# Scan stage of a decoder layer: softplus as one activation per pair, the product u moved, and another split of the products with C

## The chip, the cores and the metric

One NeuronCore of a Trainium2 chip. Its engines run their own instruction streams and meet at semaphores: TensorE (PE), VectorE (DVE), ScalarE (ACT), GpSimd (POOL), and SyncE (SP), whose queue starts most DMAs. The metric is the device time of one execution in microseconds (us).

## The reference

The layer is a Mamba block, then cross-attention, then a feed-forward block, for 16 sequences of 224 rows and 512 columns. The change is in the Mamba block:

```python
x = silu(causal_conv(hidden @ W_in)[first half])      # 1024 channels
x_dbl = x @ W_x                                       # 64 columns for dt, 16 for B, 16 for C
dt = softplus(x_dbl[..., :64] @ W_dt + b_dt)
A = -exp(A_log)                                       # 1024 x 16
# over the 224 rows of a sequence:
h = exp(dt_t[..., None] * A) * h + (dt_t * x_t)[..., None] * B_t[:, None, :]
y_t = einsum('bdn,bn->bd', h, C_t)
out = ((y + x * D) * silu(z)) @ W_out
```

## The kernel before

`mamba_phase` handles one sequence b after the other (B = 16). The scan of one sequence is cut into 32 **slots** g, four to each of the 8 channel tiles; a slot holds 32 channels times 16 states on 128 partitions and four rows of states. So there are 512 slots, and 32 of them are called a **window** here. Each engine's program is one loop over slots, and it works strictly in its own order. While the scan of sequence b runs, the same window prepares sequence b+1 (and the beginning of b+2): the tables FIRST, SECOND and LATER say in which slot each step is put. LATER is given relative to slot 4 of the sequence's own scan, so an entry `at` stands in slot 36 + at of the window before (from -36 up).

The work of one slot g:
- GpSimd, `inputs` (L811): hs[g % 8] = u times B, one product of 128x896. The ring has RING = 8 buffers; the buffer of slot g is free when TensorE has summed the tile of slot g-8, so `inputs(g)` waits for that sum.
- ScalarE, `decays` (L443): four exponentials into one of two PSUM buffers (DA = 2), one slot ahead.
- VectorE, `scan_states` (L700): the scan, and for three of four slots the product with C (L707). For every fourth slot GpSimd makes that product in `times_c` (L818), five slots later in its own order.
- TensorE, `sum_states` (L323), at every fourth slot: it sums the finished tile over the states. In its order it is followed by that slot's other matmuls.

The starts of these sums are used as marks: **M1** is the sum at slot 4 of a window (its tile is slots 0 to 3), M2 that at slot 8, up to M8, which is the next window's slot 0. M(k+1) can't come before all products with C of tile k are done, nor before TensorE has worked through what its program puts between the two.

The preparation in a usual window, by slot: x_dbl (L354) at 3 after silu of x (L518, ScalarE, slot 2); dt matmuls (L363) at 6, 8, 10, 12; for each pair of tiles a softplus in parts: Abs, Relu, Exp and Square on ScalarE (L542 to L547, `softplus_parts`), two instructions on VectorE (L687, L690, `softplus_series`), Ln and Relu on ScalarE (`softplus_log`), and at 18 one sum for all tiles on GpSimd (L823, `softplus_sum`); u = dt times x (L829, `scale_x`) at 20; store_du at 21; the gate of the sequence before (L834) on GpSimd at 8; out_proj (L375) at 11 and 13; x and z projections (L345) at 19, 21, 23, ... 31 and at 1; the transposes of the next h (L334) at 17. Between them stand 11 units of the key and value projections (L400 for keys, L404 for values), by the list `usual`. All these matmuls but the sums share three PSUM banks in turn (`take_bank`): a bank is free when its reader has run. ScalarE takes a projection out one slot after TensorE's slot (`kept_at`, and the entries tap and keep_z); `older_taps` (L674) on VectorE adds the other taps of the convolution.

SyncE's loop is in slot order too. In slot s (a multiple of 4) it loads a tile of dt and u, spread over the partitions (rep, L895), for the tile two after; the load of a sequence's first tile, in slot 24, waits for the whole store of dt and u (`du_out`).

## Time and profile before

| | |
|---|---|
| median of 3 runs | 3470.42 us (3466.92 to 3472.16) |
| the profiled execution | 3465.96 us |
| its span, first to last instruction | 3464.6 us |
| mean granted TensorE clock | 0.969 of full speed |
| busy: PE, DVE, ACT, POOL | 3157.1, 2651.0, 2391.0, 1805.6 us |

The scan stage fills the first 56% of the span, from the first scan at 84.59 us to the last sums near 1922 us; attention and feed-forward follow and are not touched. In a timeline a row gives the start in us, the duration in us, engine, line, operation, output<-input, the number of merged instructions and, in brackets, the idle time before with what ended it. In the groups of instructions the figures behind the bar are busy us and mean ns of one.

### The profile page before, as it was taken

Reading aid. Unit: us, or ns where it says so; the run is one execution under the profiler, and the core shown is the slowest. Engines: PE = TensorE matmul, PEld = TensorE weight load, DVE = VectorE, ACT = ScalarE, POOL = GpSimd, SP = SyncE. Lnnn points to the kernel's source line nnn. Section 1 sums busy time; section 2 is a strip of 40 time slices with the busy share of each in tenths; the row PEclk is TensorE's granted clock in tenths of the full one; section 3 lists DMA queues with packets and bytes.
Section 4 is the critical chain, followed back from the end, with each engine's and each line's share of the span. In section 5 each row is a group of like instructions: output and inputs, shape, how many; then the busy total and the mean of one; then the engine's idle time right before and its main releaser. Section 6 shows DMA issues by size and latency. Waiting matters only on the chain. (4 is left out here: it accounts for less than half of the span.)

```text
span 3464.6 us, 59578 instructions
## 1 busy us (share of the span) xinstructions
PE 3157.1 (91%) x20736; PEld 2191.5 (63%) x20736; DVE 2651.0 (77%) x4673; ACT 2391.0 (69%) x5339; POOL 1805.6 (52%) x1211
## 2 busy tenths in 40 slices
PE   5789889988899898988899799999999999899999
PEld 4566556665666566655655466666666666578887
DVE  2899999999999999999987577777777777523232
ACT  5778887788777877788775477777777777622222
POOL 2678888888788878887877000000010010055554
PEclk8899999999999999999999899999999999999999
DMA  5576666766676667766566221121121121120110
GB/s 164 158 188 184 179 167 175 192 185 173 154 196 189 169 155 191 194 165 166 165 186 183 87 72 48 65 76 48 53 88 48 53 86 63 52 70 25 36 38 25
DMA packets 286297, 425.01 MB, mean 123 GB/s; under 512 B 28753, under 2 KB 226129, under 8 KB 281394
## 3 DMA queue, kind: packets, MB, share of 16 engines
q1 hardware_dynamic: 278637, 411.44, 42.5%
q10 hardware_dynamic: 7365, 9.77, 0.9%
q8 instruction: 169, 2.77, 0.3%
q14 instruction: 126, 1.03, 0.1%
HBM read 320.12 MB, written 101.02 MB: 122 GB/s over the span
## 5 line engine op out<-in xcount | busy, mean ns | idle before, releaser
L811 POOL TENSOR_TENSOR a_hs<-a_rep,a_bmat 128x896 f32<-128x896 f32 x512 | 1061.7, 2097 | 282.8 <-PE a_yps L323 282.4
L443 ACT ACTIVATE a_states<-a_rep,a_a_neg 128x224 f32<-128x224 f32 x2048 | 794.6, 438 | 82.4 <-DVE a_hs L707 80.8
L700 DVE TENSOR_TENSOR_SCAN a_states<-a_states,a_hs 128x900 f32<-128x900 f32 x384 | 779.9, 2031 | 77.2 <-ACT a_states L443 62.2
L1427 DVE CUSTOM_DVE_ANT_0 b_sc<-sps,early_mask 112x375 f32<-112x375 f32 x1024 | 500.0, 545 | 133.4 <-PE sps L1173 127.4
L1314 ACT ACTIVATE b_sc<-b_sc,b_nmax 112x750 f32<-112x750 f32 x512 | 467.3, 913 | 0.7 <-DVE b_nmax L1433 0.7
L1187 PEld LDWEIGHTS b_tps<-ident,b_sc 112*125 112x125 f32 x3072 | 356.9, 189 | 168.5 <-issue 118.6
L345 PE MATMUL a_work<-early_scan_hT,w_in 128*128 128x224 f32 x2048 | 425.3, 363 | 7.5 <-issue 5.0
L707 DVE TENSOR_TENSOR a_hs<-a_states,a_cmat 128x896 f32<-128x896 f32 x384 | 419.2, 1092 | 13.2
L1187 PE MATMUL b_tps<-ident,b_sc 112*125 112x112 f32 x3072 | 404.2, 281 | 26.5 <-DVE b_pT L1441 21.0
L1567 POOL TENSOR_SCALAR b_x_var<-mv 112x2 f32<-112x2 f32 x16 | 3.4, 214 | 814.7 <-DVE mv L1478 814.7
L345 PEld LDWEIGHTS a_work<-early_scan_hT,w_in 128*128 128x128 f32 x2048 | 396.6, 196 | 49.3 <-issue 42.3
L1322 ACT ACTIVATE b_pT<-b_tps 125x448 f32<-125x448 f32 x512 | 275.6, 538 | 162.5 <-PE b_tps L1187 156.3
L400 PE MATMUL a_work<-ctx,a_wk 128*128 128x250 f32 x1536 | 351.1, 381 | 14.4 <-ACT kv_out L490 14.4
L404 PE MATMUL a_work<-wv,ctx 128*125 128x512 f32 x768 | 353.9, 604 | 9.8 <-ACT kv_out L487 9.4
L323 PE MATMUL a_yps<-a_hs,a_fold 128*32 128x224 f32 x4096 | 244.8, 383 | 114.1 <-POOL a_hs L818 46.1
L400 PEld LDWEIGHTS a_work<-ctx,a_wk 128*128 128x128 f32 x1536 | 291.6, 192 | 65.9 <-issue 17.2
L1820 ACT ACTIVATE c_g<-sps,early_b,early_alpha 128x512 f32<-128x512 f32 x112 | 87.2, 779 | 278.5 <-PE sps L1746 272.7
L1856 DVE CAST c_gT_hi<-c_g 128x512 fp32r<-128x512 f32 x112 | 66.8, 596 | 276.4 <-ACT c_g L1820 276.4
L700 DVE TENSOR_TENSOR_SCAN a_hs<-a_states,a_hs 128x900 f32<-128x900 f32 x128 | 258.9, 2023 | 25.2 <-ACT a_states L443 25.1
L323 PEld LDWEIGHTS a_yps<-a_hs,a_fold 128*32 128x32 f32 x4096 | 133.5, 115 | 225.3 <-DVE a_hs L707 96.7
L375 PE MATMUL a_work<-a_w_out,a_yT 128*112 128x512 f32 x512 | 238.8, 622 | 24.6 <-DVE early_du L690 24.6
L1894 POOL TENSOR_TENSOR c_gT_lo<-c_g,c_gT_hi 128x512 fp32r<-128x512 f32 x112 | 146.5, 1310 | 208.9 <-DVE c_gT_hi L1856 208.9
(199 smaller groups left out, 4966.4 us busy)
## 6 DMA issues: line engine op xcount, KB each, us to landing
a_rep<-du_scratch SPq DMA_DIRECT2D x512, 224.0 KB, 5.7
w_in<-W_in_dram SPq DMA_DIRECT2D x128, 512.0 KB, 4.5
du_scratch<-early_du SPq DMA_DIRECT2D x16, 1792.0 KB, 11.5
ctx<-ctxT_dram SPq DMA_DIRECT2D x48, 500.0 KB, 6.3
v_scratch<-kv_out SPq DMA_DIRECT2D x96, 250.0 KB
k_scratch<-kv_out SPq DMA_DIRECT2D x96, 250.0 KB, 4.6
b_keys<-k_scratch SPq DMA_DIRECT2D x8, 1500.0 KB, 9.2
b_v<-v_scratch SPq DMA_DIRECT2D x8, 1500.0 KB
```

Of the source, the lines that this page charges most:

```text
L323: mm = pe.matmul(yps[j * DG:(j + 1) * DG, tile % 2 * L:(tile % 2 + 1) * L], fold[:], hs[(G4 * tile + j) % RING][:, q, 1:ROW], start=(q == ...
L345: mm = pe.matmul(work[:, bank, j * L:(j + 1) * L], w_in[unit % WINS][:, k, j * P:(j + 1) * P], hT[:, k, :], start=(k == 0), stop=(k == KD ...
L400: mm = pe.matmul(work[:, bank, j * WIDE:(j + 1) * WIDE], wk[:, k, (2 * half + j) * P:(2 * half + j + 1) * P], keys[:, k, :], start=(k == 0 ...
L404: mm = pe.matmul(work[0:KC, bank, :], keys[:, k, half * KC:(half + 1) * KC], wv[:, k, :], start=(k == 0), stop=(k == KD - 1))
L443: e = act.activation(rows(states[:, g % DA, :])[:, q, 1:ROW], rep[tile % REPS][:, j, 0, :], ACT.Exp, scale=a_neg[:, g % SLOTS, q:q + 1])
L700: dve.tensor_tensor_scan(state if g % G4 else whole, state, whole, 0.0, ALU.mult, ALU.add).then_inc(S["scan"], 1)
L707: dve.tensor_tensor(hh[:, :, 1:ROW], rows(states[:, g % DA, :])[:, :, 1:ROW], cmat[b % 2][:], ALU.mult).then_inc(S["hc"], 1)
L811: pool.tensor_tensor(hs[g % RING][:, :, 1:ROW], rep[tile % REPS][:, j, 1, :].unsqueeze(1).broadcast_to([P, Q, L]), bmat[b % 2][:], ALU.mul ...
L1187: mm = pe.transpose(tps[0:KC, bank, c * TT:(c + 1) * TT], sc[buffer_of(m // 2)][:, 2 * (m % 2) + head, chunk * KC:(chunk + 1) * KC], ident ...
L1314: act.activation(scores, scores, ACT.Exp, scale=-1.0, bias=nmax[:, block % 3, j:j + 1], accum_out=esum[:, block % 2, head:head + 1]).then_ ...
L1322: act.activation(place(m, pair), transposed(tile), ACT.Copy).then_inc(S["pt_act"], 1)
L1427: dve.tensor_tensor_reduce(out=sc[buffer_of(block)][:, j, cols], in0=sps[0:TT, j, 0:HALF], in1=mask[:, block % 2, cols], scale=-1.0, scala ...
```

## The change

Softplus becomes one ScalarE activation for each pair of tiles, from PSUM into dt. In a usual window all four stand in slot 21, the dt matmuls in slots 18, 18, 21 and 21; the table of activations is switched before the first and back after the last. The parts on VectorE and the sum on GpSimd are gone. u stands in slot 26, silu of z in 25, store_du in 24; z projections and their copies one slot later. Of eight products with C GpSimd takes three (slots 0, 4 and 6 of every eight) instead of two; the third stands four slots after its scan in GpSimd's order, and VectorE's scan of such a slot writes straight to the ring buffer. The key and value units keep their number, with some slots moved. For the first sequence softplus, skip, u and store_du come earlier, and the first table switch goes straight to softplus. The semaphores and the counts that are waited for follow (`products`, `pool_products`).

```diff
@@ -241,23 +238,22 @@
             "row_stats": [-65], "squares": [-60], "guess": [-58], "gains": [-54], "h": [-53], "hT": [-51], "keep_hT": [-50],
             "load_x": [-67, -66, -48, -47], "load_z": [-46, -45, -28, -28], "x": spaced(-49, 1), "tap": spaced(-48, 1),
             "older_taps": spaced(-47, 1), "z": [-30, -29, -24, -23], "keep_z": [-29, -28, -23, -22], "residual": [-19],
-            "silu_x": [-43], "x_dbl": [-42], "xd": [-41], "store_bc": [-41], "dt": spaced(-40, 1), "parts": spaced(-39, 1),
-            "series": spaced(-38, 1), "logs": spaced(-37, 1), "skip": [-32, -31], "spread": [-28], "dt_sum": [-30],
-            "silu_z": [-20], "u": [-28], "store_du": [-27]}
+            "silu_x": [-43], "x_dbl": [-42], "xd": [-41], "store_bc": [-41], "dt": [-40, -40, -40, -39],
+            "softplus": [-39, -39, -39, -39], "skip": [-42, -42], "spread": [-38], "silu_z": [-20], "u": [-38],
+            "store_du": [-37]}
         SECOND = {
             "load": [-20], "row_stats": [-16], "squares": [-15], "guess": [-14], "gains": [-13], "h": [-12], "hT": [-11],
             "keep_hT": [-10], "load_x": [-7, 1, 3, 5], "load_z": [-6, 2, 4, 6], "x": spaced(0, 2), "tap": spaced(1, 2),
             "older_taps": spaced(2, 2), "z": spaced(1, 2), "keep_z": spaced(2, 2), "residual": [9], "silu_x": [9],
-            "x_dbl": [10], "xd": [11], "store_bc": [11], "dt": spaced(12, 1), "parts": spaced(13, 1),
-            "series": spaced(14, 1), "logs": spaced(15, 1), "skip": [18, 19], "spread": [17], "dt_sum": [20],
-            "silu_z": [21], "u": [21], "store_du": [22]}
+            "x_dbl": [10], "xd": [11], "store_bc": [11], "dt": [18, 18, 21, 21],
+            "softplus": [21, 21, 21, 21], "skip": [18, 19], "spread": [17], "silu_z": [25], "u": [26], "store_du": [24]}
         LATER = {
             "load": [-68], "row_stats": [-64], "squares": [-60], "guess": [-58], "gains": [-54], "h": [-53], "hT": [-51],
             "keep_hT": [-50], "load_x": spaced(-52, 4), "load_z": spaced(-50, 4), "x": spaced(-49, 4), "tap": spaced(-48, 4),
-            "older_taps": spaced(-47, 4), "z": spaced(-47, 4), "keep_z": spaced(-46, 4), "residual": [-35], "silu_x": [-34],
-            "x_dbl": [-33], "xd": [-32], "store_bc": [-32], "dt": spaced(-30, 2), "parts": spaced(-29, 2),
-            "series": spaced(-28, 2), "logs": spaced(-27, 2), "skip": [-20, -19], "spread": [-19], "dt_sum": [-18],
-            "silu_z": [-16], "u": [-16], "store_du": [-15]}
+            "older_taps": spaced(-47, 4), "z": spaced(-46, 4), "keep_z": spaced(-45, 4), "residual": [-35], "silu_x": [-34],
+            "x_dbl": [-33], "xd": [-32], "store_bc": [-32], "dt": [-18, -18, -15, -15],
+            "softplus": [-15, -15, -15, -15], "skip": [-20, -19], "spread": [-19], "silu_z": [-11], "u": [-10],
+            "store_du": [-12]}
         when = [FIRST, SECOND] + [{name: [b * SLOTS + BEHIND + at for at in slots_of] for name, slots_of in LATER.items()}
                                   for b in range(2, B)]
 
@@
...
-        usual = (1, 3, 5, 12, 14, 18, 20, 22, 24, 26, 30)
+        usual = (1, 3, 5, 12, 13, 18, 20, 21, 24, 25, 29)
...
@@ -281,9 +277,16 @@
 
         bank_of = {}
 
+        def pool_multiplies(g):
+            return g % (2 * G4) in (0, G4, G4 + 2)
+
         def products(g):
 
-            return (G4 - 1) * (g // G4) + g % G4
+            return 5 * (g // (2 * G4)) + sum(not pool_multiplies(n) for n in range(g % (2 * G4) + 1))
+
+        def pool_products(g):
+
+            return 3 * (g // (2 * G4)) + sum(pool_multiplies(n) for n in range(g % (2 * G4) + 1))
 
         def in_unit(b, name, pair):
 
@@ -314,8 +317,8 @@
                 return bank
 
             def sum_states(tile):
-                pe.wait_ge(S["hc"], (G4 - 1) * (tile + 1))
-                pe.wait_ge(S["hc_pool"], tile + 1)
+                pe.wait_ge(S["hc"], products(G4 * tile + G4 - 1))
+                pe.wait_ge(S["hc_pool"], pool_products(G4 * tile + G4 - 1))
                 if tile % 2 == 0 and tile:
                     pe.wait_ge(S["y"], tile // 2)
                 for q in range(Q):
@@ -435,7 +438,7 @@
                 tile, j = g // G4, g % G4
                 if j == 0:
                     act.wait_ge(S[f"rep{tile % REPS}"], 16 * G4 * (tile // REPS + 1))
-                if g >= DA and (g - DA) % G4 == 0:
+                if g >= DA and pool_multiplies(g - DA):
                     act.wait_ge(S["scan"], g - DA + 1)
                 elif g >= DA:
                     act.wait_ge(S["hc"], products(g - DA))
@@ -516,7 +519,7 @@
                     act.wait_ge(S["du_out"], 16 * b)
                 for half in halves:
                     act.activation(xs[:, half, :], conv[:, half, :], ACT.Silu).then_inc(S["xs"], 1)
-                act.preload_act_table_set("natural_log_exp_and_others")
+                act.preload_act_table_set("natural_log_exp_and_others" if b else "softplus")
 
             def silus_z(b):
                 act.wait_ge(S["z"], PAIRS * (b + 1))
@@ -533,29 +536,16 @@
                 act.activation(xd[0:R, :], work[0:R, bank, 0:L], ACT.Copy).then_inc(S["xd"], 1)
                 act.activation(bc[R:R + 2 * N, :], work[R:R + 2 * N, bank, 0:L], ACT.Copy).then_inc(S["bc"], 1)
 
-            def softplus_parts(b, pair):
-                n = PAIRS * b + pair
-                cols = slice(2 * pair, 2 * pair + 2)
-                view = pair_of_tiles("dt", b, pair)
-                act.wait_ge(S["dt_ps"], n + 1)
+            def softplus(b, pair):
+                act.wait_ge(S["dt_ps"], PAIRS * b + pair + 1)
                 act.wait_ge(S["xs"], 2 * (b + 1))
-                steps.after(act.activation(conv[:, cols, :], view, ACT.Abs))
-                steps.after(act.activation(dt[:, cols, :], view, ACT.Relu))
-                steps.settle()
-                steps.after(act.activation(conv[:, cols, :], conv[:, cols, :], ACT.Exp, scale=-1.0))
-                steps.settle()
-                act.activation(view, conv[:, cols, :], ACT.Square, scale=3.0 ** -0.5,
-                               bias=series_bias[:]).then_inc(S["square"], 1)
-
-            def softplus_log(b, pair):
-                n = PAIRS * b + pair
-                cols = slice(2 * pair, 2 * pair + 2)
-                act.wait_ge(S["part"], n + 1)
-                steps.after(act.activation(conv[:, cols, :], conv[:, cols, :], ACT.Ln, bias=1.0))
-                steps.settle()
-                act.activation(conv[:, cols, :], conv[:, cols, :], ACT.Relu, bias=log_small[:]).then_inc(S["log_part"], 1)
+                act.activation(dt[:, 2 * pair:2 * pair + 2, :], pair_of_tiles("dt", b, pair),
+                               ACT.Softplus).then_inc(S["dt"], 1)
+                if pair == PAIRS - 1:
+                    act.preload_act_table_set("natural_log_exp_and_others")
 
             def skip(b, half):
+                act.wait_ge(S["xs"], 2 * b + half + 1)
                 if b >= 2:
                     act.wait_ge(S["o_ps"], 2 * (b - 1))
                 for m in range(half * M // 2, (half + 1) * M // 2):
@@ -817,14 +785,9 @@
                 pool.wait_ge(S["scan"], g + 1)
                 pool.tensor_tensor(hh[:, :, 1:ROW], hh[:, :, 1:ROW], cmat[b % 2][:], ALU.mult).then_inc(S["hc_pool"], 1)
 
-            def softplus_sum(b):
-                pool.wait_ge(S["part"], PAIRS * (b + 1))
-                pool.wait_ge(S["log_part"], PAIRS * (b + 1))
-                pool.tensor_tensor(dt, dt, conv[:], ALU.add).then_inc(S["dt"], 1)
-
             def scale_x(b):
                 pool.wait_ge(S["skip"], 2 * (b + 1))
-                pool.wait_ge(S["dt"], b + 1)
+                pool.wait_ge(S["dt"], PAIRS * (b + 1))
                 pool.wait_ge(S["xd_ps"], b + 1)
                 pool.tensor_tensor(xs, xs, dt, ALU.mult).then_inc(S["u"], 1)
 
@@ -851,14 +814,13 @@
             for slot in range(slots[0], ALL + 50):
                 if 0 <= slot < ALL:
                     inputs(slot)
-                if 0 <= slot - AHEAD < ALL and (slot - AHEAD) % G4 == 0:
-                    times_c(slot - AHEAD)
+                for g in (slot - AHEAD, slot - AHEAD + 1):
+                    if 0 <= g < ALL and pool_multiplies(g) and (g % G4 == 0) == (g == slot - AHEAD):
+                        times_c(g)
                 for b, _ in due(slot, "squares"):
                     squares_of(b)
                 for b, _ in due(slot, "gains"):
                     gains(b)
-                for b, _ in due(slot, "dt_sum"):
-                    softplus_sum(b)
                 for b, _ in due(slot, "u"):
                     scale_x(b)
                 for b in range(B - 1):
```

## Rows read from the trace of the kernel before

**Rows 1.** page, part 2: busy tenths of VectorE in 40 slices of the span

```profile
DVE  2899999999999999999987577777777777523232
```

**Rows 2.** timeline of TensorE in one window: start us, duration us, engine, line, [idle before]

```profile
907.62 3.24 PE L354 MATMUL a_work<-early_du,early_w_x 128*96 128x224 f32 x16 [0.75 <-ACT early_du L518]
910.79 1.74 PE L323 MATMUL a_yps<-a_hs,a_fold 128*32 128x224 f32 x32
...
915.94 0.92 PE L363 MATMUL a_work<-a_xd,early_w_dt 65*128 65x224 f32 x4
...
923.64 1.74 PE L323 MATMUL a_yps<-a_hs,a_fold 128*32 128x224 f32 x32 [3.35 <-POOL a_hs L818]
...
934.13 7.12 PE L375 MATMUL a_work<-a_w_out,a_yT 128*112 128x512 f32 x16 [3.47 <-DVE early_du L690]
941.18 1.73 PE L323 MATMUL a_yps<-a_hs,a_fold 128*32 128x224 f32 x32
...
952.07 1.73 PE L323 MATMUL a_yps<-a_hs,a_fold 128*32 128x224 f32 x32 [1.34 <-DVE a_hs L707]
...
969.14 2.62 PE L323 MATMUL a_yps<-a_hs,a_fold 128*32 128x224 f32 x32 [3.04 <-issue]
...
982.13 1.74 PE L323 MATMUL a_yps<-a_hs,a_fold 128*32 128x224 f32 x32
983.80 3.65 PE L400 MATMUL a_work<-ctx,a_wk 128*128 128x250 f32 x16
987.28 3.19 PE L345 MATMUL a_work<-early_scan_hT,w_in 128*128 128x224 f32 x16
990.31 3.60 PE L404 MATMUL a_work<-wv,ctx 128*125 128x512 f32 x8
...
996.86 1.74 PE L323 MATMUL a_yps<-a_hs,a_fold 128*32 128x224 f32 x32
```

**Rows 3.** timeline of TensorE, the same product seven windows later

```profile
1703.40 3.24 PE L354 MATMUL a_work<-early_du,early_w_x 128*96 128x224 f32 x16 [0.80 <-ACT early_du L518]
```

**Rows 4.** timeline of GpSimd in the window of group 2

```profile
912.70 2.10 POOL L811 TENSOR_TENSOR a_hs<-a_rep,a_bmat 128x896 f32<-128x896 f32 x1 [2.17 <-PE a_yps L323]
...
919.53 2.08 POOL L811 TENSOR_TENSOR a_hs<-a_rep,a_bmat 128x896 f32<-128x896 f32 x1
921.57 1.93 POOL L818 TENSOR_TENSOR a_hs<-a_hs,a_cmat 128x896 f32<-128x896 f32 x1
...
967.12 1.92 POOL L818 TENSOR_TENSOR a_hs<-a_hs,a_cmat 128x896 f32<-128x896 f32 x1
```

**Rows 5.** costly groups of VectorE in that window: busy us, mean ns, idle before

```profile
L707 DVE TENSOR_TENSOR a_hs<-a_states,a_cmat 128x896 f32<-128x896 f32 x24 | 26.2, 1092 | 0.8
...
L687 DVE SCALAR_TENSOR_TENSOR a_work<-a_work,early_conv 128x448 f32<-128x448 f32 x4 | 2.5, 615 | 0.0
```

**Rows 6.** costly groups of ScalarE in that window

```profile
L543 ACT ACTIVATE early_du<-a_work 128x448 f32<-128x448 f32 x4 | 2.1, 532 | 0.0
...
L518 ACT ACT_TABLE_LOAD x1 | 1.3, 1283 | 0.0
```

**Rows 7.** timeline of TensorE early on, after a longer wait

```profile
124.42 6.06 PE L354 MATMUL a_work<-early_du,early_w_x 128*96 128x224 f32 x16 [6.24 <-ACT early_du L518]
```

**Rows 8.** DMA issues: KB each and median us to landing

```profile
a_rep<-du_scratch SPq DMA_DIRECT2D x512, 224.0 KB, 5.7
...
du_scratch<-early_du SPq DMA_DIRECT2D x16, 1792.0 KB, 11.5
```

**Rows 9.** timeline of the prologue, ScalarE and GpSimd

```profile
44.23 0.55 ACT L542 ACTIVATE early_conv<-a_work 128x448 f32<-128x448 f32 x1 [0.80 <-PE a_work L363]
...
61.99 3.99 POOL L829 TENSOR_TENSOR early_du<-early_du 128x1792 f32<-128x1792 f32 x1
```

**Rows 10.** timeline of TensorE in the last window

```profile
1851.38 1.73 PE L323 MATMUL a_yps<-a_hs,a_fold 128*32 128x224 f32 x32
...
1860.10 1.73 PE L323 MATMUL a_yps<-a_hs,a_fold 128*32 128x224 f32 x32
```

More of the change, by code:

```diff
@@ L16 @@
 NEG_INF_SCALE = -1e9
-LOG1P_SMALL = 2.0 ** -8
 class Memory:
@@ L234, in mamba_phase @@
         n_weights = 11
-        n_const = 6
+        n_const = 4
         def spaced(first, step):
@@ L358, in dt_raw @@
             def dt_raw(b, pair):
-                bank = take_bank(("dt", b, pair), "part", PAIRS * b + pair + 1)
+                bank = take_bank(("dt", b, pair), "dt", PAIRS * b + pair + 1)
                 pe.wait_ge(S["xd"], b + 1)
@@ L638, in scalar_program @@
                     keep_xd(b)
-                for b, pair in due(slot, "parts"):
-                    softplus_parts(b, pair)
-                for b, pair in due(slot, "logs"):
-                    softplus_log(b, pair)
+                for b, pair in due(slot, "softplus"):
+                    softplus(b, pair)
                 for b, _ in due(slot, "silu_z"):
@@ L681, in older_taps @@
                 e.then_inc(S["conv"], 1)
-            def softplus_series(b, pair):
-                cols = slice(2 * pair, 2 * pair + 2)
-                series = pair_of_tiles("dt", b, pair)
-                dve.wait_ge(S["square"], PAIRS * b + pair + 1)
-                steps.after(dve.scalar_tensor_tensor(out=series, in0=series, scalar=13.0 / 16.0, in1=conv[:, cols, :],
-                                                     op0=ALU.add, op1=ALU.mult))
-                steps.settle()
-                dve.scalar_tensor_tensor(
-                    out=dt[:, cols, :], in0=series, scalar=LOG1P_SMALL * (LOG1P_SMALL ** 2 / 3 - LOG1P_SMALL / 2 + 1),
-                    in1=dt[:, cols, :], op0=ALU.min, op1=ALU.add).then_inc(S["part"], 1)
             def scan_states(g):
@@ L762, in vector_program @@
                     dve.tensor_scalar(a_neg[:], a_neg[:], -1.0, None, ALU.mult).then_inc(S["const"], 1)
-                    dve.wait_ge(S["log_small"], 1)
-                    steps.after(dve.tensor_scalar(log_small[:], log_small[:], -1.0, None, ALU.mult))
-                    steps.settle()
                 for b, pair in due(slot, "older_taps"):
                     older_taps(b, pair)
-                for b, pair in due(slot, "series"):
-                    softplus_series(b, pair)
                 for b in range(B):
```

28 lines of the change are left out of this document (11 added, 17 removed).

## Prediction

> **What bounds the kernel now.** I read the page first. Its row of slices shows VectorE busy at 90% or more through the whole scan, slices 3 to 18 of 40 [rows 1]. Taken alone that says: every microsecond taken off VectorE is a microsecond gained. So I went on to the timeline of one window, engine by engine, to see which wait ends last at each mark. One x_dbl starts at 907.62 us and the one seven windows later at 1703.40 [rows 2, 3]: 795.78 / 7 = 113.7 us for a window. The marks inside are the starts of the sums [rows 2]:
>
> M1 910.79, M2 923.64, M3 941.18, M4 952.07, M5 969.14, M6 982.13, M7 996.86.
>
> What ended each stretch is to be read from the idle time in brackets and from what ran just before:
> - M1 to M2, 12.85 us: TensorE idles 3.35 us for GpSimd. The chain is GpSimd's own. Its first product of the stretch starts 1.91 us after the sum did (912.70, the ring buffer comes free); small steps and the gate follow, the next product at 919.53, the product with C from 921.57 to 923.50, and the sum starts at 923.64 [rows 2, 4].
> - M2 to M3, 17.54: TensorE. It waits 3.47 us for a bank that the softplus series on VectorE holds, then out_proj takes 7.12 and ends at the mark.
> - M3 to M4, 10.89: VectorE's last product, with 1.34 of waiting.
> - M4 to M5, 17.07: GpSimd again. Its product with C ends at 967.12 + 1.92 = 969.04, late because the softplus sum and u stand before it on its engine [rows 4].
> - M5 to M6, 12.99, and M6 to M7, 14.73 (M7 to M8 is its like): TensorE without a gap. 14.73 is a sum, two units and two projections [rows 2].
>
> So VectorE ends one of eight stretches, though it looks full. TensorE and GpSimd end most. TensorE couples back within about a slot: ScalarE must take out what TensorE made one slot earlier before it makes the next decays.
>
> **The change part by part**, against the profiled execution (3465.96 us; span 3464.6). From [rows 2]: a key unit takes 3.48 (983.80 to 987.28), a value unit 3.6, so 3.5 each; a projection 3.03 (987.28 to 990.31); a sum 1.67 (982.13 to 983.80); the two dt matmul pairs of one step 0.85 (0.92 with their tail); out_proj 7.1.
>
> VectorE loses four pairs of instructions at 615 ns (the second of each pair is put at the price of the first) and 4 of 24 products at 1092 ns [rows 5]: 4.9 + 4.4 = 9.3 us a window. ScalarE loses 24 activations and gains 4 of the length of a Relu from PSUM, 0.53, with two table loads of 1.28 [rows 6]. GpSimd loses a sum of 4.0 and gains four products of 1.93: +3.7 us [rows 4]. None of that counts by itself; the stretches do:
>
> 1. M1 to M2. Tile 1 is an odd one, so the mark now needs two products on GpSimd, at slots 9 and 10, and between them stands one more `inputs`. The chain grows by 2.07 + 1.93 [rows 4]: 12.85 + 4.0 = **16.85**. No cover is left: TensorE has 1.67 + 2 x 3.5 = 8.7 us of work there and VectorE about 11.5. **+4.0**.
> 2. M2 to M3. The dt matmuls and their bank wait are gone: sum, unit and out_proj give 1.67 + 3.5 + 7.1 = 12.3. But TensorE comes out of a wait of 16.85 - 8.7 = 8.2 us. What that does is seen earlier: after 6.24 us of idling x_dbl took 6.06 us, against 3.24 in the usual window [rows 7, 2], and the sum after 3.04 idle took 2.62 for 1.74. This is the granted clock at its lower level, 1.2 for 2.4 GHz. The loss was 2.8 and 0.9; for 8.2 us I take 2.6, bounds 0 and 5.6 (twice the row, since the wait is longer). 14.9 against 17.54: **-2.6**.
> 3. M3 to M4. VectorE's work falls below, but tile 3 is odd: release of the buffers 1.91, three `inputs`, two products: 1.91 + 3 x 2.07 + 2 x 1.93 = 12.0, against 10.89: **+1.1**. This is a floor for every stretch that ends an odd tile.
> 4. M4 to M5. The softplus sum and u no longer stand in GpSimd's chain. TensorE is next: sum, two units, transposes of 0.9, two dt steps, one projection: 1.7 + 7.0 + 0.9 + 1.7 + 3.1 = 14.4, with 0.6 for banks that wait for ScalarE: 15.0. **-2.1**.
> 5. M5 to M6. Work: sum, two dt steps, z, unit, x: 1.7 + 1.7 + 3.0 + 3.5 + 3.1 = 13.0. The third dt step needs the bank of the first, which the first softplus frees; on ScalarE that is behind a tap of the x projection (1.0), the decays (1.6), the table load (1.28) and the softplus (0.55): 4.6 us after M5 with its latencies, where TensorE is ready at 1.7. So it stands for 3.0, and everything queued behind it (dt, z, unit, x) moves. 16.1 against 12.99: **+3.1**. The table load back costs ScalarE 1.28, and the decays wait, but TensorE is later still.
> 6. M6 to M8 and M8 to M1 stay: the same matmuls, full clock. u has moved to slot 26; there GpSimd has some 3 us to spare in each stretch. store_du in slot 24 holds SyncE until u is done, some 16 us after M5, and what is queued behind it (a w_in load, key and value stores, then rep, which needs the store's 11.5 us and 5.7 of its own [rows 8]) still lands about when the ring asks for it, near M7 + 2. I put it at 0, bounds 0 and +2.
>
> Sum for a usual window: 4.0 - 2.6 + 1.1 - 2.1 + 3.1 = +3.5 against this window's 113.0; against the mean of 113.7, which holds the windows where the clock was low already, +2.8. Thirteen usual windows: **+36**. The last two: each gets step 1 (+4), their matmul work is the same, and in the last the stretch from 1851.38 to 1860.10, 8.72 us [rows 10], rises to the 12.0 of step 3; less about 2 for the lighter steps: **+11**. In the prologue the first softplus starts at 44.23 [rows 9] and four of 0.53 with the last dt step end near 47.3, so u ends at 51.3 instead of 61.99 + 3.99 = 65.98. Not all of the 14.7 us arrives: the z projections, their silu and the next sequence's first steps on ScalarE stand before the first decays. Half is taken, **-7**, bounds -14.7 and 0. First window: 0, bounds -5 and +5.
>
> Total +40: 3466 + 40 = 3506 for such an execution. That execution was 4.5 us below the median of the runs, so **3510**.
>
> A rule that speaks against step 5's size: in the Trainium skill, "ScalarE: Activation LUTs", section "Rules for kernel authors", a switch to a different set is budgeted at about 2.7 us. The trace has 1283 ns for one load [rows 6]. With the page's figure the stand of TensorE would be 1.4 us longer in each window, an estimate of 18 us more in all, 3528; I go by the row.
>
> **The rivals.**
> (a) *The clock costs nothing more than before*, because TensorE's waits only change places. For: the windows before hold low stretches already. Against: 8.2 us is longer than any wait in the usual window, and the work behind it is now what sets M3. Then step 2 is -5.2, the window +0.2 against the mean: 13 x 0.2 + 11 - 7 = +7, **3477**, give or take 15.
> (b) *TensorE doesn't stand in slot 21*, as it is late enough, or ScalarE early enough, to meet the softplus, and the clock holds. Step 5 then gives 13.0 and step 2 12.3, so the window is 2.9 below the mean: 13 x -2.9 + 4 = -34, **3436**. This ends on the other side. Its place is slot 21; with the clock held it decides from the point where that wait is under some 2.5 us, with the loss of step 2 never.
> (c) *VectorE was the bound*: the 90% are true and the waits at the marks only follow it. Then 9.3 us go from 15 windows, 140, and with the prologue 147: **3324**. Against it stands that M2 and M5 end on GpSimd's product to within 0.14 us and M6 and M7 on TensorE without a gap.
> (d) *Slower than forecast*: the rep load of the next sequence comes late (2 us a window) and the clock falls at three waits rather than one (0.9 more twice): 13 x 3.8 = 49, **3559** at the end. It is the tail of the forecast, not a case of its own.
> That softplus isn't one activation, or needs more tables than counted, would show at once in slot 21 and costs 1.28 for each load more.
>
> **How the numbers follow.** Forecast 0.53, (a) 0.24, (b) 0.12, (c) 0.11. The time is the forecast's, 3510. A difference under 0.2% (7 us) is about what a measurement of this kernel can't tell from none. The forecast lies above that with nearly all its chance. (a) spreads 3462 to 3492: a third within 0.2%, a tenth below. So faster 0.12 + 0.11 + 0.03 = 0.26; same 0.09; slower 0.65. For 8 in 10 the range leaves out (c) and the last of (d): **3430 to 3550**.
>
> **What would show it.** In a window of the profile after: M1 to M2 at 16.8 with TensorE idle 8 us for GpSimd's product with C; a granted clock of 0.5 behind it and out_proj or unit stretched; M3 to M4 at 12; M4 to M5 near 15 with no wait on GpSimd; in M5 to M6 a wait of 3 us of the dt matmul for ScalarE; M6 to M8 at 14.7 each; VectorE's share of the scan falling from over 90% to about 85% with the window no shorter. It would be wrong if GpSimd's third product were not in the mark's chain, or if the marks moved together with VectorE's instruction sum.

## The result, and the profile after

The changed kernel takes 3550.39 us (median of 4 runs, 3548.5 to 3551.32) where the kernel before takes 3470.35 (3466.92 to 3472.16, runs on the same chip): ratio 1.0231, 95% interval 1.0213 to 1.0249. That is 80 us slower. The forecast was 3510, with the sign right and half of the size missing; 3550.39 is just above its range.

The page of the kernel after, rows of busy tenths and of the granted clock in 40 slices:

```profile
DVE  2888788878887888788877477777777777622222
...
PEclk8899889988998999899999899999999999999999
```

VectorE has fallen from 9 to 7 and 8 [rows 1], and the clock row has many slices of 8. For the scan, 200 to 1700 us, here is the view of one stretch: us, then busy time (with instruction records) of PE, PEld, DVE, ACT and POOL, then granted clock, DMA share and GB/s. First the kernel after:

```profile
200.00:1700.00 1500.00, 1316.24 (x7369) 906.46 (x7372) 1247.67 (x1078) 1054.96 (x2445) 1235.20 (x708) 0.91 0.66 168
```

The kernel before, the same stretch:

```profile
200.00:1700.00 1500.00, 1346.64 (x7769) 928.35 (x7758) 1419.39 (x1298) 1211.36 (x2799) 1245.21 (x696) 0.96 0.66 177
```

In these 1500 us VectorE is busy 172 us less and ScalarE 156, but part of that is only that fewer windows fit into them. Over the same thirteen usual windows (226.02 to 1703.40 us before, 217.81 to 1770.52 after) VectorE's busy time falls from 1399 to 1289 us, which is 8.5 us a window where 9.3 were forecast, and ScalarE's from 1196 to 1091; the windows take 75 us more. What moved is the clock, 0.96 to 0.91, and the marks. The timeline of TensorE in one window of the kernel after (columns as in [rows 2]):

```profile
934.34 3.24 PE L357 MATMUL a_work<-early_du,early_w_x 128*96 128x224 f32 x16 [0.28 <-ACT early_du L521]
937.51 1.74 PE L326 MATMUL a_yps<-a_hs,a_fold 128*32 128x224 f32 x32
...
954.29 3.21 PE L326 MATMUL a_yps<-a_hs,a_fold 128*32 128x224 f32 x32 [8.03 <-POOL a_hs L786]
957.44 4.90 PE L403 MATMUL a_work<-ctx,a_wk 128*128 128x250 f32 x16
962.18 7.03 PE L378 MATMUL a_work<-a_w_out,a_yT 128*112 128x512 f32 x16
969.14 1.74 PE L326 MATMUL a_yps<-a_hs,a_fold 128*32 128x224 f32 x32
...
981.15 3.05 PE L326 MATMUL a_yps<-a_hs,a_fold 128*32 128x224 f32 x32 [3.22 <-POOL a_hs L786]
...
996.64 1.74 PE L326 MATMUL a_yps<-a_hs,a_fold 128*32 128x224 f32 x32
1001.08 3.36 PE L366 MATMUL a_work<-a_xd,early_w_dt 65*128 65x224 f32 x8 [2.69 <-ACT early_du L542]
1004.23 4.96 PE L348 MATMUL a_work<-early_scan_hT,w_in 128*128 128x224 f32 x16
1009.02 3.60 PE L407 MATMUL a_work<-wv,ctx 128*125 128x512 f32 x8
1012.46 3.19 PE L348 MATMUL a_work<-early_scan_hT,w_in 128*128 128x224 f32 x16
1015.58 1.74 PE L326 MATMUL a_yps<-a_hs,a_fold 128*32 128x224 f32 x32
```

Three waits stand in it: 8.03 us before M2, 3.22 before M4, both for GpSimd's product with C, and 2.69 behind M5 for the first softplus. Behind each of them the matmuls are longer than their like: the sum takes 3.21 and 3.05 for 1.74, the key unit 4.90 for 3.65, the dt step 3.36 for 1.68, the projection 4.96 for 3.19. The granted clock of the five stretches from M1 to M6, same kernel, columns as above:

```profile
937.50:954.30 16.80, 8.77 (x58) 5.43 (x58) 16.39 (x13) 12.19 (x34) 14.90 (x11) 0.87 0.71 162
954.30:969.10 14.80, 14.80 (x64) 8.24 (x64) 11.07 (x8) 7.08 (x20) 12.99 (x13) 0.81 0.44 108
969.10:981.20 12.10, 8.88 (x53) 3.77 (x56) 11.37 (x9) 9.32 (x23) 10.44 (x7) 0.97 0.93 204
981.20:996.60 15.40, 15.40 (x88) 11.31 (x88) 9.41 (x8) 8.60 (x23) 11.98 (x6) 0.91 0.44 136
996.60:1015.60 19.00, 16.31 (x85) 12.64 (x84) 13.17 (x13) 12.61 (x26) 15.93 (x7) 0.82 0.55 166
```

GpSimd in the stretch before M2, same kernel:

```profile
939.42 2.09 POOL L779 TENSOR_TENSOR a_hs<-a_rep,a_bmat 128x896 f32<-128x896 f32 x1 [1.69 <-PE a_yps L326]
...
942.32 3.98 POOL L797 TENSOR_TENSOR a_yT<-a_yT,a_zs 128x1792 f32<-128x1792 f32 x1
946.27 2.07 POOL L779 TENSOR_TENSOR a_hs<-a_rep,a_bmat 128x896 f32<-128x896 f32 x1
948.30 1.93 POOL L786 TENSOR_TENSOR a_hs<-a_hs,a_cmat 128x896 f32<-128x896 f32 x1
950.18 2.09 POOL L779 TENSOR_TENSOR a_hs<-a_rep,a_bmat 128x896 f32<-128x896 f32 x1
952.23 1.93 POOL L786 TENSOR_TENSOR a_hs<-a_hs,a_cmat 128x896 f32<-128x896 f32 x1
```

It doesn't wait once after 939.42 (the three rows not shown there take 0.2 us each). The last product ends at 952.23 + 1.93 = 954.16 and the sum starts at 954.29. Against [rows 4] the chain has one `inputs` and one product with C more, 2.07 + 1.93.

The stretches, as means of twelve usual windows (us), with the forecast of each. The last row is the mean of the twelve windows that begin one later, so it can differ from the column's sum by a tenth or two:

| | before | forecast | after |
|---|---|---|---|
| M1 to M2 | 12.86 | 16.85 | 16.81 |
| M2 to M3 | 18.17 | 14.9 | 14.88 |
| M3 to M4 | 10.95 | 12.0 | 12.02 |
| M4 to M5 | 17.03 | 15.0 | 15.59 |
| M5 to M6 | 12.78 | 16.1 | 18.84 |
| M6 to M7, M7 to M8 | 14.73 each | 14.73 | 14.73 each |
| M8 to M1 | 12.31 | 12.3 | 11.84 |
| window, from x_dbl to x_dbl | 113.70 | 116.5 | 119.47 |

### The profile page after: what moved, and what is told of

Read it like the earlier page. It is cut to its first block and busy times, and to the rows that moved or that the text cites. A ratio compares the mean times of both kernels' runs of the same rounds, so it can differ in the third digit from the quotient of the medians.

```text
span 3550.0 us, 59151 instructions
## 1 busy us (share of the span) xinstructions
PE 3198.6 (90%) x20736; PEld 2224.3 (63%) x20736; DVE 2512.9 (71%) x4478; ACT 2261.1 (64%) x5049; POOL 1862.7 (52%) x1259
## 5 line engine op out<-in xcount | busy, mean ns | idle before, releaser
L675 DVE TENSOR_TENSOR_SCAN a_states<-a_states,a_hs 128x900 f32<-128x900 f32 x320 | 649.2, 2029 | 175.3 <-ACT a_states L446 174.4
L348 PE MATMUL a_work<-early_scan_hT,w_in 128*128 128x224 f32 x2048 | 432.6, 370 | 12.2 <-issue 9.7
L675 DVE TENSOR_TENSOR_SCAN a_hs<-a_states,a_hs 128x900 f32<-128x900 f32 x192 | 388.7, 2024 | 68.8 <-ACT a_states L446 52.7
L348 PEld LDWEIGHTS a_work<-early_scan_hT,w_in 128*128 128x128 f32 x2048 | 411.9, 202 | 38.0 <-issue 27.9
L326 PE MATMUL a_yps<-a_hs,a_fold 128*32 128x224 f32 x4096 | 264.6, 407 | 180.4 <-POOL a_hs L786 171.1
L786 POOL TENSOR_TENSOR a_hs<-a_hs,a_cmat 128x896 f32<-128x896 f32 x192 | 371.0, 1932 | 7.8 <-DVE a_hs L675 7.8
L403 PE MATMUL a_work<-ctx,a_wk 128*128 128x250 f32 x1536 | 361.4, 389 | 5.9 <-ACT kv_out L493 5.9
L682 DVE TENSOR_TENSOR a_hs<-a_states,a_cmat 128x896 f32<-128x896 f32 x320 | 349.2, 1091 | 11.0
```

Of the source, the lines that this page charges most:

```text
L326: mm = pe.matmul(yps[j * DG:(j + 1) * DG, tile % 2 * L:(tile % 2 + 1) * L], fold[:], hs[(G4 * tile + j) % RING][:, q, 1:ROW], start=(q == ...
L348: mm = pe.matmul(work[:, bank, j * L:(j + 1) * L], w_in[unit % WINS][:, k, j * P:(j + 1) * P], hT[:, k, :], start=(k == 0), stop=(k == KD ...
L403: mm = pe.matmul(work[:, bank, j * WIDE:(j + 1) * WIDE], wk[:, k, (2 * half + j) * P:(2 * half + j + 1) * P], keys[:, k, :], start=(k == 0 ...
L675: dve.tensor_tensor_scan(whole if pool_multiplies(g) else state, state, whole, 0.0, ALU.mult, ALU.add).then_inc(S["scan"], 1)
L682: dve.tensor_tensor(hh[:, :, 1:ROW], rows(states[:, g % DA, :])[:, :, 1:ROW], cmat[b % 2][:], ALU.mult).then_inc(S["hc"], 1)
L786: pool.tensor_tensor(hh[:, :, 1:ROW], hh[:, :, 1:ROW], cmat[b % 2][:], ALU.mult).then_inc(S["hc_pool"], 1)
```

## The experiments

Theories at this point. **T1**: the path goes from mark to mark, the third product costs because it is in an odd tile's chain on GpSimd, and the rest of the miss is the low clock behind TensorE's waits. **T2**: the three-of-eight split is harmless and the softplus block with its two table loads is what costs. **T3**: GpSimd has too much work, wherever the product stands.

**Each part alone.** The kernel after with GpSimd's two old products (and the counts 6 and 2 of eight in `products` and `pool_products`):

```diff
-            return g % (2 * G4) in (0, G4, G4 + 2)
+            return g % (2 * G4) in (0, G4)
```

> The changed kernel with GpSimd taking two of eight products with C again (slots 0 and 4), softplus and u as changed. Theory A (GpSimd's third product in the chain of the odd marks costs 4 us at M2 and 1 to 2 us at M4, and TensorE's wait before M2 brings the low clock behind it): M1 to M2 falls from 16.8 to 12.85, M2 to M3 from 14.85 to 12.3 to 14, M3 to M4 from 12.0 to about 10.5, the window from 119.4 to 112 +- 1.5 us, the total from 3550 to 3445 (3420 to 3470). Rival B (the loss is the softplus block in slot 21, which holds ScalarE and TensorE): only the 4 us at M2 go, the rest turns up in the following stretches, M5 to M6 stays at 18.9 and the window stays above 115: total above 3485. Rival C (VectorE bound): VectorE has 4.4 us more per window, so no gain at all: 3550 or more.

Measured: 3412.03 us, ratio to before 0.9834 [0.9817, 0.985]; window 110.33. That is under the expected 3420 to 3470: M3 to M4 came out at 9.41, where 10.5 was expected.

The other half is the kernel before with `pool_multiplies`, `pool_products` and the loop of `times_c` of the change, and nothing else.

> The kernel before with only the split of the products with C changed to three of eight (slots 0, 4, 6), softplus in parts as before. Theory A: M1 to M2 rises from 12.85 to 16.85, M3 to M4 from 10.9 to 12.0; M2 to M3 loses part of its 3.5 us bank wait as the series on VectorE is done by then, but gets the low clock: about 16 to 17. M4 to M5 with softplus sum and u in the chain and an even tile stays at 17. Window about 117 to 118 against 113.7, total 3470 + 15 x 3.5 = 3522 (3495 to 3550). Rival C (VectorE bound): it loses 4.4 us of work per window, total 3470 - 66 = 3404.

Measured: 3532.8 us, 1.0179 [1.0164, 1.0194]; window 117.19. T2 falls. But the halves don't add: -60 and +61 us make +1, and together they measure +80. The means of the stretches say why:

| | M1-M2 | M2-M3 | M3-M4 | M4-M5 | M5-M6 | window |
|---|---|---|---|---|---|---|
| before | 12.86 | 18.17 | 10.95 | 17.03 | 12.78 | 113.70 |
| before + split | 16.78 | 16.29 | 12.02 | 15.95 | 14.08 | 117.19 |
| after, old split | 12.95 | 13.99 | 9.41 | 14.79 | 17.85 | 110.33 |
| after | 16.81 | 14.88 | 12.02 | 15.59 | 18.84 | 119.47 |

On top of before, the split takes 3.9 us in M1-M2, 1.1 in M3-M4, 1.3 in M5-M6 (where TensorE now waits for GpSimd's product at M6) and 0.5 in M6-M7, and gets 1.9 and 1.1 back in M2-M3 and M4-M5. Why those two give back was not tested: the likely reason is that the bank wait for the series and the sum in GpSimd's order ran out while the chain was late anyway. With softplus in one piece those stretches are short already. Nothing is given back, M3-M4, which VectorE had let fall to 9.41, is held up at 12.02 (+2.6), and the split costs 9.1 us a window instead of 3.5.

**Place or amount.** The same number of products on GpSimd, the third in an even tile, which ends at M1, M3, M5 or M7:

```diff
-            return g % (2 * G4) in (0, G4, G4 + 2)
+            return g % (2 * G4) in (0, 2, G4)
```

> The changed kernel with GpSimd's third product moved from slot 6 to slot 2 of every eight, so that the two products stand in the chain of the even tiles, whose stretches (M2 to M3, M4 to M5, M6 to M7) TensorE already fills with more than 12 us. The number of products of each engine is that of the changed kernel. Theory A: M1 to M2 falls to 12.85, M2 to M3 to 12.3 to 14, M3 to M4 to 10 to 10.5, the others stay; window 111 to 112.5, total 3550 - 14 x 7.5 = 3440 (3420 to 3465). Rival D (GpSimd's sheer amount of work is the bound, 99.7 us a window, wherever the products stand): no change, 3550 within 15. Rival B (softplus block): above 3485.

Measured: 3413.27 us, 0.9837 [0.9822, 0.9852]; window 110.04, M1-M2 12.97, M2-M3 14.42, M3-M4 9.20. That is 137 us less than the kernel after with not one instruction fewer. T3 falls. That is also 27 us below the expected 3440: M3-M4 fell under the level of before, as VectorE's lighter load allows once GpSimd's chain doesn't hold it. It is no faster than the old split, though: what VectorE is spared ends no stretch.

**The chain before M2.** The gate, 3.98 us on GpSimd, goes behind the two products:

```diff
-                    if slot == (b + 1) * SLOTS + 8:
+                    if slot == (b + 1) * SLOTS + 11:
```

> The changed kernel with three of eight products on GpSimd as changed (slots 0, 4, 6), but the gate of the sequence before (4.0 us) moved on GpSimd from slot 8 to slot 11, behind the products of that mark. Theory A (it is the sum of what stands in GpSimd's chain between M1 and M2): M1 to M2 falls from 16.8 to 12.8, out_proj then waits for the gate until about 19 us after M1, so M3 comes at 26 instead of 31.6 after M1, M4 at 38 instead of 43.6; window -5 to -5.6, total 3550 - 14 x 5.3 = 3475 (3460 to 3500). Rival D (GpSimd's amount of work is the bound): no change.

Measured: 3498.78 us, 1.0072 [1.0057, 1.0087]. M1-M2 is 12.93, so the gate's 3.9 us were in the chain. M3-M4 rose to 13.19 and M4-M5 to 16.96, where the gate now stands in the way. The expected 3475 was too low, for TensorE's wait before M2 is still 4.09 us, and it still comes out of it at the low clock:

```profile
930.78 3.22 PE L326 MATMUL a_yps<-a_hs,a_fold 128*32 128x224 f32 x32 [4.09 <-POOL a_hs L786]
933.92 4.95 PE L403 MATMUL a_work<-ctx,a_wk 128*128 128x250 f32 x16
...
958.37 3.22 PE L326 MATMUL a_yps<-a_hs,a_fold 128*32 128x224 f32 x32 [3.93 <-DVE a_hs L682]
961.52 4.86 PE L407 MATMUL a_work<-wv,ctx 128*125 128x512 f32 x8
```

**The clock by itself.** If it is the clock, then TensorE kept busy in its waits must give the time back although it does more. Matmuls whose result nobody reads are put where it waits; the computation is whole and unchanged. The first try, 32 of them in slot 7:

```diff
...
+                for k in range(count):
+                    pe.matmul(work[:, bank, 0:250], wk[:, k % KD, 0:P], wk[:, k % KD, 128:378], start=True, stop=True)
...
+                if SLOTS < slot < ALL - SLOTS and slot % SLOTS == 7:
+                    fill(32)
```

> The changed kernel with 32 extra matmuls of 250 columns (about 7 us at full clock, results never read) at the end of slot 7 of 14 windows, in the 8 us in which TensorE waits for GpSimd's product before M2. Nothing else is changed. Clock theory: TensorE no longer idles there, so the granted clock stays at full and the sum and unit behind M2 take 1.7 and 3.5 us in place of 3.2 and 4.9; M1 to M2 stays at 16.8, M2 to M3 falls from 14.85 to 12.3 and the later stretches stay; window 119.4 to 117, total 3550 - 14 x 2.5 = 3515 (3505 to 3530). Rival (the wait itself, by the chain on GpSimd, is all that counts and the matmuls behind it are hidden): no gain, and up to 10 us of loss where the extra work is late: 3550 to 3560.

Measured: 3592.64 us, 1.0344 [1.0329, 1.036]. The filler was mis-sized. Timeline of TensorE in this kernel:

```profile
961.42 13.66 PE L387 MATMUL a_work<-a_wk 128*128 128x250 f32 x64
975.00 1.74 PE L326 MATMUL a_yps<-a_hs,a_fold 128*32 128x224 f32 x32
```

It took 13.66 us where 7 were meant, and M1-M2 grew to 22.17. The row says why: 32 of these matmuls stand in it as x64 records, two for each, so the 16 records of a key unit (3.5 us) are eight matmuls and one costs 0.43 us, not 0.22. Yet M2-M3 was 12.14, near the 12.3 that the prediction put down for full clock. So the filler was cut to 15 (`fill(15)`):

> The changed kernel with the filling of slot 7 cut to size. The kernel before this one showed that 32 extra matmuls take 13.7 us, not 7, so they were late themselves (M1 to M2 22.2), but behind them the sum and unit ran at full clock and M2 to M3 was 12.1 in place of 14.85. With 15 of them (6.4 us) TensorE is done before GpSimd's product. Clock theory: M1 to M2 16.8, M2 to M3 12.3, M3 to M4 12.0, M4 to M5 still 15.5, M5 to M6 17.3 to 18.9; total 3550 - 14 x 2.5 = 3515 (3495 to 3525). Rival: 3550 or more.

Measured: 3508.26 us, 1.0113 [1.0098, 1.0128]. 42 us less than the kernel after by doing more. M1-M2 16.92, M2-M3 12.13. Next 7 more in slot 13, before M4:

> The same with 7 more extra matmuls (3.0 us) at the end of slot 13, in the 3.2 us in which TensorE waits before M4. Clock theory: M4 to M5 falls too, from 15.5 to 14.2, and M5 to M6 stays near 17.3, where its own wait of 2.7 us comes with a low clock: total 3550 - 14 x (2.5 + 1.3 + 1.6) = 3474 (3465 to 3500). Rival: no more than the kernel with slot 7 alone filled.

Measured: 3497.53 us, 1.0083 [1.0068, 1.0098]. M4-M5 fell from 15.44 to 14.29, but M5-M6, which was to fall too, stayed at 18.54. The miss is useful: with both waits ahead of it filled, the 2.69 us wait in slot 21 still brings the low clock. Where it sets in varies from window to window of this one program: the dt step behind the same wait takes from 2.0 to 3.4 us, and M5-M6 is 17.3 in three of the twelve windows and about 18.9 in nine. Last, 12 short matmuls into the free columns of `yps`, ahead of the third dt step in slot 21:

```diff
+                if SLOTS < slot < ALL - SLOTS and slot % SLOTS == 21:
+                    fill_beside_sums(12)
```

> As the kernel with slots 7 and 13 filled, and 12 extra matmuls of 64 columns (results never read) between the sum of slot 20 and the third dt matmul, in the 2.7 us in which TensorE waits for the first softplus. Clock theory: the wait itself stays, but the dt matmuls (3.36 us for 1.7) and the z projection (4.96 for 3.2) behind it run at full clock, so M5 to M6 falls from 18.5 to 15.7 to 16.1, the size that the prediction gave this stretch; total 3497.5 - 14 x 2.6 = 3461 (3450 to 3475). Rival (M5 to M6 is long for another reason, the decays held behind the softplus block): M5 to M6 stays above 18, total 3490 or more.

Measured: 3457.72 us, 0.9966 [0.9956, 0.9976], clock 0.984, window 112.25. Timeline of TensorE behind M5 in this kernel:

```profile
952.68 1.74 PE L326 MATMUL a_yps<-a_hs,a_fold 128*32 128x224 f32 x32
954.36 2.89 PE L391 MATMUL a_yps<-a_wk 128*128 128x64 f32 x24
957.12 1.78 PE L366 MATMUL a_work<-a_xd,early_w_dt 65*128 65x224 f32 x8
958.73 3.19 PE L348 MATMUL a_work<-early_scan_hT,w_in 128*128 128x224 f32 x16
```

The dt step still starts 4.44 us behind M5, as in the kernel after (996.64 to 1001.08), because the bank comes no sooner. But it takes 1.78 for 3.36 and the projection 3.19 for 4.96. M5-M6 is 15.60. All three waits filled, 3550 has become 3458: 93 us of the changed kernel are clock, of which the forecast held 34 (2.6 in thirteen windows).

**The stand in slot 21.** Softplus and the last two dt matmuls one slot earlier, where no decays stand between the tap and the table load (the second sequence's table is moved in the same way):

```diff
...
-            "x_dbl": [-33], "xd": [-32], "store_bc": [-32], "dt": [-18, -18, -15, -15],
-            "softplus": [-15, -15, -15, -15], "skip": [-20, -19], "spread": [-19], "silu_z": [-11], "u": [-10],
+            "x_dbl": [-33], "xd": [-32], "store_bc": [-32], "dt": [-18, -18, -16, -16],
+            "softplus": [-16, -16, -16, -16], "skip": [-20, -19], "spread": [-19], "silu_z": [-11], "u": [-10],
```

> The changed kernel with softplus and the last two dt matmuls of a sequence one slot earlier, in slot 20, so that ScalarE doesn't make the decays between the tap and the table load (1.6 us); the split of the products stays at slots 0, 4, 6. Theory: the stand of TensorE behind M5 falls from 2.7 to about 1.2 us, and with it the low clock behind it (sum 1.7, dt 3.36 for 1.7, projection 4.96 for 3.2): M5 to M6 from 18.9 to 14.5 to 16, window -3 to -4, total 3550 - 14 x 3.5 = 3500 (3485 to 3520). Rival (that wait only takes slack that M6 to M8 would otherwise have had to wait for, VectorE or GpSimd next in line): under 10 us, 3540 or more.

Measured: 3507.64 us, 1.0107 [1.0092, 1.0122]; M5-M6 16.51, a little over the expected 14.5 to 16. TensorE's wait behind M5 fell to 1.24 us as expected, and a second one of 0.74 stands before the projection, which still takes 4.95. With the even split as well:

> The changed kernel with both corrections: GpSimd's third product in the even tiles (slot 2) and softplus in slot 20. If the two losses are in different stretches they add: 3413 - 42 = 3371 at best; but with the split moved, M5 to M6 has lost part of its low clock already (17.3 against 18.9), so 1.3 us less per window: 3413 - 20 = 3390 (3375 to 3400). Rival (VectorE is next in line, 99.8 us of work in windows of 109 us): no gain over 3413.

Measured: 3396.43 us, 0.9774 [0.9757, 0.9791]; window 108.68. Slot 20 still gains, but 17 us where it gained 43 with the odd split: M5-M6 falls by 1.4 rather than 2.3, and M2-M3 not at all rather than by 1.1. Why M2-M3 had gained there is left open.

Then softplus in the stretch M1-M2, slots 6 and 7, where TensorE has 8 us to wait in the kernel after and some 4 with the even split. This kernel has the even split; the second sequence's softplus moves to slot 14 and the last one's stays in slot 21:

```diff
...
-            "x_dbl": [-33], "xd": [-32], "store_bc": [-32], "dt": [-18, -18, -15, -15],
-            "softplus": [-15, -15, -15, -15],
+            "x_dbl": [-33], "xd": [-32], "store_bc": [-32], "dt": [-30, -30, -29, -29],
+            "softplus": [-29, -29, -29, -29],
```

> The changed kernel with GpSimd's third product in the even tiles and softplus (with its dt matmuls) in slots 6 and 7, where TensorE waits 4 us for the gate's chain anyway, and not in slots 18 to 21, where TensorE is the bound; only for the last sequence it stays in slot 21. Theory (the stretch in which work stands decides, not its amount): M1 to M2 stays at 13, M2 to M3 at 12.3 to 14, M4 to M5 falls from 14.2 to 12.5 to 13, M5 to M6 from 17.3 to 12.5 to 13.5, the window to 104 to 106; total 3413 - 13 x 5.5 = 3341 (3325 to 3365). Rival (VectorE, 99.8 us of work, or ScalarE's block of 5.4 us in slot 7 holds M2): M1 to M2 rises to 15 or more and the total stays above 3375.

Measured: 3400.39 us, 0.9806 [0.9789, 0.9822]. The expectation of 3325 to 3365 failed, and the rival's two signs came. M5-M6 fell to 11.72 as meant, and M1-M2 rose to 19.79. From its timeline:

```profile
992.64 1.02 PE L369 MATMUL a_work<-a_xd,early_w_dt 65*128 65x224 f32 x4 [2.24 <-ACT kv_out L496]
997.00 1.86 PE L369 MATMUL a_work<-a_xd,early_w_dt 65*128 65x224 f32 x4 [3.34 <-ACT early_du L545]
998.65 4.85 PE L406 MATMUL a_work<-ctx,a_wk 128*128 128x250 f32 x16
...
1002.35 2.04 DVE L678 TENSOR_TENSOR_SCAN a_states<-a_states,a_hs 128x900 f32<-128x900 f32 x1 [3.91 <-ACT a_states L449]
```

The stand moved along with the block: two waits for banks, 2.24 and 3.34, a key unit queued behind them at the low clock, and a scan that waits 3.91 for decays behind the softplus. The new place had looked free because TensorE waited there; ScalarE, which must empty the banks, was not free. In the same place with the change's own odd split:

> The same place of softplus (slots 6 and 7), but GpSimd's third product left in the odd tiles (slot 6) as in the changed kernel. Theory: M1 to M2 16.8, M2 to M3 12.3 to 14.9, M3 to M4 12.0, M4 to M5 13 to 14.5, M5 to M6 12 to 14, M6 to M8 14.7 each: window 111 to 113; total 3550 - 13 x 7.5 = 3450 (3430 to 3475). Against the kernel with both places corrected the split costs 8 us a window. Rival: the split is not what costs once softplus is out of TensorE's way, and this kernel is within 20 us of that one.

Measured: 3460.75 us, 0.9974 [0.9964, 0.9983]; M1-M2 18.95, window 112.41. Here that stretch was 16.81 long anyway, so the block costs 2.1 there and takes 6.8 from M5-M6. The two losses overlap instead of adding up, and against the even split in the same place the odd one costs 60 us in all, about half of the 8 us a window that were expected.

**The prologue.** One of the w_in loads for the z projections issued before the store of dt and u, not behind it:

```diff
...
-            "load_x": [-67, -66, -48, -47], "load_z": [-46, -45, -28, -28],
+            "load_x": [-67, -66, -48, -47], "load_z": [-46, -45, -38, -28],
```

> The changed kernel with the third w_in load of the first sequence issued before the store of dt and u in SyncE's order, not behind it. In the changed kernel TensorE waits 7.6 us in the prologue for the w_in loads that land together with that store, and the first scan starts at 83.6, only 1 us earlier than before. Theory (the store delays them): that wait falls to 2 to 5 us and the first scan starts at 78 to 81, total 3 to 5 us less than the changed kernel's. Rival (the matmuls there wait for something else): first scan at 83.6 again.

Measured, in one execution: 3547.78 us; the first scan at 81.61, against 83.62 in the kernel after. TensorE's wait fell from 7.60 to 4.17. From the timelines, first the kernel after:

```profile
47.58 3.99 POOL L792 TENSOR_TENSOR early_du<-early_du 128x1792 f32<-128x1792 f32 x1 [35.28 <-ACT early_du L542]
...
51.59 0.35 SPq L848 DMA_DIRECT2D du_scratch<-early_du  x1
51.99 1.46 SPq L891 DMA_DIRECT2D w_in<-W_in_dram  x2
...
60.52 8.86 PE L348 MATMUL a_work<-early_scan_hT,w_in 128*128 128x224 f32 x32 [7.60 <-issue]
```

Then this kernel:

```profile
52.14 0.43 SPq L891 DMA_DIRECT2D w_in<-W_in_dram  x1
52.69 0.43 SPq L848 DMA_DIRECT2D du_scratch<-early_du  x1
...
58.20 9.18 PE L348 MATMUL a_work<-early_scan_hT,w_in 128*128 128x224 f32 x32 [4.17 <-issue]
```

The wait is for those loads, at least in good part: 3.4 us of it went, 2.0 reached the first scan, a little less than expected. In the total, 2 us can't be told from nothing. Which share of the rest is the store's traffic wasn't separated.

**A version that beats both.** Even split, softplus in slot 20, and 5 short fillers there:

> The fastest kernel so far (third product in the even tiles, softplus in slot 20; M5 to M6 at 16.35, with a wait of 1.24 us and one of 0.74) with 5 extra matmuls of 64 columns ahead of the third dt step. Clock theory: z behind it takes 3.2 in place of 4.95 us, M5 to M6 14.6 to 15, total 3396 - 14 x 1.5 = 3375 (3365 to 3385). Rival (the wait is too short to be what lowers the clock): 3396 within 5.

Measured: 3379.19 us, 0.9743 [0.9727, 0.9759], 91 us faster than before and 171 faster than after. M5-M6 is 15.29. Before M2 its TensorE still waits 4.13 us and comes out with a sum of 3.22, which wasn't filled in any run with this split.

## Why the prediction was right or wrong

**What bounds the kernel: right.** The path ran from mark to mark. VectorE lost 8.5 us of work in each window and the window grew by 5.8. Rival (c), 3324, is out, and the two splits with equal VectorE relief (3413 and 3550) show it a second time. The one stretch that VectorE had ended, M3 to M4, did fall with it, to 9.2 and 9.4, in the two splits where GpSimd's chain doesn't hold it. (The row of busy tenths reads 9 from slice 3 to 20, not to 18; nothing hangs on that.)

**Step 1, +4.0: right.** 16.81 for 16.85, with the wait (8.03 for 8.2), and the chain is shown from two sides: without the third product M1 to M2 is 12.95, and with the gate out of it 12.93. **Step 2, 14.9: right in sum and in both terms.** 12.13 with the wait filled, so 2.75 of clock where 2.6 was taken. Rival (a), no further cost of the clock, is out. **Step 3, 12.0: right** (12.02); with the two other splits the stretch is 9.20 and 9.41.

**Step 4, 15.0: two errors that half cancel.** TensorE's work there is 14.29, as the run with two fillers shows, so the 0.6 for banks wasn't needed; and the 3.22 us wait before M4 costs 1.3 of clock, which the step left out though it had raised that wait itself: 12.0 long, with 8.9 of work. Together +0.6.

**Step 5, +3.1: the mechanism right, the term mis-sized, and this is the main miss.** The first softplus was to free the bank 4.6 us behind M5; it was 4.44, and TensorE stood 2.69 us for 3.0. Rows of ScalarE in slot 21 of the kernel after (M5 at 996.64), and VectorE's next scan:

```profile
999.19 1.28 ACT L542 ACT_TABLE_LOAD   x1
...
1000.48 0.98 ACT L542 ACTIVATE early_du<-a_work 128x448 f32<-128x448 f32 x2
...
1004.47 0.54 ACT L542 ACTIVATE early_du<-a_work 128x448 f32<-128x448 f32 x1 [0.95 <-PE a_work L366]
...
1005.03 1.28 ACT L545 ACT_TABLE_LOAD   x1
...
1007.92 2.04 DVE L675 TENSOR_TENSOR_SCAN a_states<-a_states,a_hs 128x900 f32<-128x900 f32 x1 [3.98 <-ACT a_states L446]
```

At full clock the stretch is 15.60 (the run with three fillers), 0.5 under the forecast. It measured 18.84: 3.2 us are the low clock over dt step and projection, for which the step had nothing. So the step is 2.7 a window too low, 36 of the 45 us by which the profiled execution passed 3506. The prediction knew from [rows 7, 2] what such a wait does and charged it once, at M2, where the wait was longest; its tail (d) had "0.9 more twice". The two waits that it left out cost 1.3 and 3.2. By the budget of about 2.7 us for a switch that the Trainium skill gives ("ScalarE: Activation LUTs", section "Rules for kernel authors"), the switch would have made the stand 1.4 longer, an estimate. The trace doesn't agree: the load took 1.28, the first softplus started right behind it at 1000.48, and the stand was shorter than forecast, so the row was the right choice.

**Step 6: right.** 14.73 twice. M8 to M1 gained 0.5. Holding the store back to slot 24 cost nothing that shows; it landed in a median of 6.2 us for 11.5 [rows 8], and why it was faster wasn't looked into.

**Sum of a window:** +0.6 + 2.7 - 0.5 + 0.1 of rounding = 2.9 over the forecast, times 13 = 38 us. **Prologue, -7: wrong by 6.** u ended at 51.57, 0.3 us from the forecast, and the first scan came only 1.0 sooner (83.62 for 84.59). The step looked at ScalarE's queue and not at SyncE's, where the w_in loads stand right behind the store that it had moved forward. The run with one load ahead of the store gave back 2.0 of these 6 us; the rest is open. **First window, 0, and the last two, +11: two errors that cancel.** From the first scan to the third x_dbl (226.02 us before, 217.81 after) the kernel after takes 7.2 us less, outside the step's bounds of -5 and +5. The thirteen windows from there (to 1703.40 and 1770.52) take 75.3 more, and what follows, the last two and the rest, 18.3 more where 11 was forecast. Together -1.0 - 7.2 + 75.3 + 18.3 = 85.4, the difference of the two profiled executions. That these two terms came to the forecast's 11 in sum is luck, so 38 + 6 make 44 of the 45. Neither term was tested by a run.

**Rival (b)** needed TensorE not to stand in slot 21. It stood. Its place was right all the same: the slot-20 runs gained there. The steps priced each stretch with both halves of the change in it, so what the halves do to each other was in the sum, but neither half was priced alone. That is what decides here: softplus alone would have been a gain of 60 us.

## What to carry to other kernels

In a loop of in-order engines, find which wait ends last at each mark, and ask of an instruction that moves to a less busy engine in which mark's chain it will stand: the same product cost 9 us a window in the odd tiles and nothing in the even ones. Charge every wait that a change adds or leaves on TensorE, not only the longest, with the clock of the matmuls behind it, and test it by filling the wait with matmuls that nobody reads. When a change has two parts, work the sum of each alone: one had hidden most of the other's price.
